# Layer 0's dense product in matmuls of 256 columns instead of 512

## What is computed

```python
def _L0_cond_ref(x, condition, weights):
    W = weights[condition]
    return jnp.einsum('bct,bcd->bdt', x, W)

def _L0_ffn_ref(x, W_base, b_base, enc0, enc1, coefs0, coefs1, mask0, mask1):
    base = jnp.einsum('bsd,od->bso', x, W_base) + b_base
    ...
    transformed = real_fourier_orthogonal_multiply(decoded)
    update = transformed.sum(axis=0)
    return base + update * SCALING

def _L1_ffn_ref(x, kernel, scale):
    w = kernel.astype(x.dtype) * 2.0 - 1.0
    return scale * jnp.einsum('bsi,if->bsf', x, w)

x = x + _L0_ffn_ref(_L0_cond_ref(x, itok_B_0_15, L0_cond_weights), ...)
x = x + _L1_ffn_ref(_L1_cond_ref(x, itok_B_0_30, L1_cond_weights), ...)
```

## Time and profile before

| | |
|---|---|
| median of 3 runs | 227.8 us (227.55 to 227.83) |
| profiled execution | 227.68 us |
| its span, first to last instruction | 225.5 us |
| TensorE busy (matmuls) | 220.1 us, 98%, 1212 records |
| weight loads | 185.2 us, 82%, 1212 records |
| POOL, DVE, ACT busy | 110.1, 98.8, 75.0 us |

### The profile page before, as it was taken

How to read it: one execution, slowest core, us unless ns; L and a number is a source line. 1 busy time by engine, 2 the same in 40 slices (tenths; PEclk the granted TensorE clock), 3 DMA queues, 4 the chain that set the end, 5 groups by cost and what they waited for, 6 DMA issues and landing times.

```text
span 225.5 us, 3597 instructions
## 1 busy us (share of the span) xinstructions
PE 220.1 (98%) x1212; PEld 185.2 (82%) x1212; DVE 98.8 (44%) x147; ACT 75.0 (33%) x199; POOL 110.1 (49%) x133
## 2 busy tenths in 40 slices
PE   7799999999999999999999999999999999999995
PEld 2568888888888888888888888888888888888884
DVE  4246444344544343445443444454434444544334
ACT  2067233333322333333223333332233333322211
POOL 4757754355566545445665454456654544522200
PEclk9999999999999999999999999999999999999999
DMA  6931022333222323322233323221232332212112
GB/s 201 310 99 52 9 96 96 102 93 84 72 53 96 99 96 99 99 63 88 52 96 99 96 99 99 71 81 52 96 99 96 99 99 81 73 49 90 47 49 93
DMA packets 13543, 20.42 MB, mean 91 GB/s; under 512 B 2618, under 2 KB 4538, under 8 KB 13538
## 3 DMA queue, kind: packets, MB, share of 16 engines
q1 hardware_dynamic: 10642, 18.16, 25.3%
q0 software_dynamic: 2048, 1.05, 2.4%
q10 hardware_dynamic: 848, 1.14, 1.5%
HBM read 11.96 MB, written 8.39 MB: 90 GB/s over the span
## 4 chain that ended last, share of the span: by engine, by line
PE 95%; DMA 3%; DVE 0%; ACTq 0%; issue 0%
PE f_ps L443 26%; PE y_ps L423 26%; PE f_ps L453 13%; PE f_ps L460 13%; PE f_ps L465 13%; DMA basis_sb<-in_fourier_basis 3%; PE a_ps L481 2%; PE a_ps L408 1%; PE y_ps L417 0%; DVE x L392 0%; PE a_ps L460 0%; PE f_ps L417 0%; PE a_ps L465 0%; ACTq L260 0%; ACTq L259 0%
## 5 line engine op out<-in xcount | busy, mean ns | idle before, releaser
L224 POOL TENSOR_TENSOR x<-x_in,bias 128x512 f32<-128x512 f32 x32 | 40.9, 1278 | 81.0 <-issue 46.9
L217 POOL DMA_INDIRECT gathered<-in_L_cond_weights,row_now x58 | 56.5, 974 | 13.2 <-issue 10.1
L443 PE MATMUL f_ps<-a_high,y_high 128*128 128x512 f32 x128 | 53.8, 420 | 0.0
L443 PE MATMUL f_ps<-a_low,y_high 128*128 128x512 f32 x128 | 50.3, 393 | 0.0
L358 DVE TENSOR_TENSOR x<-f_ps,x 128x512 f32<-128x512 f32 x32 | 22.1, 692 | 49.4 <-PE f_ps L443 47.9
L286 ACT ACTIVATE y_high<-y_ps 128x512 fp32r<-128x512 f32 x32 | 19.1, 597 | 69.6 <-PE y_ps L423 69.6
L282 ACT ACTIVATE y_high<-y_ps 128x512 fp32r<-128x512 f32 x32 | 19.1, 597 | 61.4 <-PE y_ps L423 61.4
L460 PE MATMUL f_ps<-b_sign,y_high 128*128 128x512 f32 x124 | 36.5, 415 | 0.0
L423 PEld LDWEIGHTS y_ps<-blocks,x_in 128*128 128x128 f32 x256 | 33.5, 191 | 3.5 <-issue 0.7
L423 PEld LDWEIGHTS y_ps<-blocks,x 128*128 128x128 f32 x256 | 33.4, 191 | 3.2 <-DVE x L358 0.5
L453 PE MATMUL f_ps<-a_high,y_low 128*128 128x512 f32 x128 | 35.1, 396 | 0.0
(11 more groups left out here) (44 smaller groups left out, 73.0 us busy)
## 6 DMA issues: line engine op xcount, KB each, us to landing
x_in<-in_x SPq DMA_DIRECT2D x31, 256.0 KB, 2.7
out_x<-x SPq DMA_DIRECT2D x31, 256.0 KB, 2.0
gathered<-in_L_cond_weights,row_now POOLq DMA_INDIRECT x58, 2.4
w_sb<-in_L_ffn_W_base SPq DMA_DIRECT2D x1, 512.0 KB, 7.5
w_sb<-in_L_ffn_W_base ACTq DMA_DIRECT2D x1, 512.0 KB, 8.9
basis_sb<-in_fourier_basis SPq DMA_DIRECT2D x1, 257.0 KB, 3.3
basis_sb<-in_fourier_basis ACTq DMA_DIRECT2D x1, 257.0 KB, 6.7
bias<-in_L_ffn_b_base SPq DMA_DIRECT2D x1, 256.0 KB
```

What stands on the lines that cost most here:

```text
L217: nc.gpsimd.indirect_dma_start(gathered[:, slot, layer, :], None, mix_rows[layer], IndirectOffsetOnAxis(rows[:, layer:layer + 1].bitcast(u ...
L224: nc.gpsimd.tensor_tensor(out=x1[:, slot, :], in0=x_in[:, slot, :], in1=bias[:, :], op=ALU.add).then_inc(biased, 1)
L443: last = nc.tensor.matmul(f0_ps[:, :], y0_high[:, k * P:(k + 1) * P], a[:, k, :], start=(k == 0 and a is a_high), stop=(k == CHUNKS - 1 an ...
```

## The change

Every matmul of feed0 becomes two, one for columns 0 to 255 and one for columns 256 to 511 of the same bank, of the same stationary operand. The list halves stood in the kernel already. Only the very first matmul of the two halves has start=True. Feed1 and everything else stays; the lines behind feed0 move down by four.

```diff
                     for a in (a_high, a_low):
-                        last = nc.tensor.matmul(f0_ps[:, :], y0_high[:, k * P:(k + 1) * P], a[:, k, :],
-                                                start=(k == 0 and a is a_high), stop=(k == CHUNKS - 1 and a is a_low))
+                        for half, columns in enumerate(halves):
+                            last = nc.tensor.matmul(f0_ps[:, columns], y0_high[:, k * P:(k + 1) * P], a[:, k, columns],
+                                                    start=(k == 0 and a is a_high and half == 0),
+                                                    stop=(k == CHUNKS - 1 and a is a_low), skip_group_check=True)
                     return last
 ...
                 for k in range(CHUNKS):
-                    nc.tensor.matmul(f0_ps[:, :], y0_low[:, k * P:(k + 1) * P], a_high[:, k, :], start=False, stop=False)
+                    for columns in halves:
+                        nc.tensor.matmul(f0_ps[:, columns], y0_low[:, k * P:(k + 1) * P], a_high[:, k, columns],
+                                         start=False, stop=False, skip_group_check=True)
                 high(CHUNKS - 1).then_inc(fed0, 1)
```

## The result

The changed kernel takes 225.69 us (median of 4 runs, 225.04 to 226.19), the kernel before 227.81 us beside it: a ratio of 0.990 with a 95% interval of 0.987 to 0.993. It is faster by 2.1 us, where 1.0 us slower was forecast, and outside the range. Most of what the forecast said of the mechanism is in the profile; the one price on which its sign hung is not. The kernel before takes 209.3 us from its first product on, so counted like this, too, the change is worth 2.1 us.

What follows compares the result with a forecast made beforehand. The prediction took TensorE's queue of matmuls, which never runs dry, as the bound: 227.68 us profiled + 1.07 for the splits = 228.75 us, 228.87 on the median's scale, stated as 228.8, range 226.9 to 231.0.

Steps and rivals of the forecast that it cites:

- the price of a half: Layer 0's product: a 256-column matmul with its load takes 117.75 ns, read in the last tile; a split costs 2.8 ns.
- the break-even: Layer 0's product: a half at 116.35 ns, half of 232.7 ns, below which the change makes the kernel faster.
- the faster rival: Layer 0's product: halves run at the loads' pace, about 113 ns; -2.6 us, 225.1 us; chance 0.12.
- its own tests: Wrong size if halves leave 117 to 119 ns; wrong mechanism if tiles outgrow the product or queue 8 brings blocks every turn.
- 1.07 us for all 12: Layer 0's product: 384 splits at 2.8 ns each, all on TensorE's path, add 1.07 us.
- The code was not brought in again: Slower rival, TensorE's loop: longer code fetched again at each of 8 returns, 8.8 us, 237.6 us; chance 0.04.
- the 7.4 us that it would give: Layer 0's product: if the load's estimated 107 ns alone paced the halves, the kernel would gain about 7.4 us.

Runs made afterwards that it cites:

- e0: The changed kernel run once more, with no edit, timed against the kernel before: 225.98 us, ratio 0.994.
- e13: The changed kernel with the last matmul of layer 0's product left whole: 228.56 us, ratio 1.003 to the kernel before.
- e14: e13 with the last chunk of layer 1's low part in two halves: 228.63 us, ratio 1.004 to the kernel before.
- the quarters: The changed kernel with layer 0's product in four parts of 128 columns instead of two halves: 309.02 us, one execution.
- e11: The changed kernel with both layers in halves, save the last matmul of each layer's product left whole: 224.58 us, ratio 0.987 to the kernel before.
- e12: e11 with one extra matmul, once, ahead of the loop: 224.42 us, ratio 0.986 to the kernel before.
- e3: The changed kernel with layer 1's product in interleaved halves too, in all tiles but the last: 227.04 us, ratio 0.997 to the kernel before.
- e7: e3 with the last low chunk of layer 1 left whole: 226.72 us, ratio 0.997 to the kernel before.
- e8: The changed kernel with the last chunk of layer 1's low part alone in two halves: 227.22 us, ratio 0.999 to the kernel before.

## Why the prediction was wrong

**The step that failed** is the price of a half: "I take the middle, 117.75 ns", and then "I stay at 117.75, since those rows are of the very operation, eight and six in a row". The rows were read rightly, and they were of the very operation, but from one stretch, 2 us at the end, entered after a wait of TensorE's load for y1_high, and the price was carried over to 31 tiles in a full queue. There a half takes 113 to 114 ns: the product is 2.74 us, 2.74 / 24 = 114.2 ns with its entry, so a split gains 232.7 - 228.3 = 4.4 ns and 384 of them 1.7 us. With the 0.01 us that layer 1's product is shorter in each tile (1.86 instead of 1.87 us), 0.3 us in all, that is the measured 2.1 us within the spread of the runs.

That the stretch read 118 seems to be partly luck of the one execution that was profiled: in the changed kernel the same stretch has read both ways. The halves of line 464 in the last tile, without the first and the last one, read as follows in its first profile and then in e0:

```profile
219.12 0.87 PE L464 MATMUL a_ps<-b_sign,y_high 128*128 128x256 f32 x6
```

```profile
217.90 0.84 PE L464 MATMUL a_ps<-b_sign,y_high 128*128 128x256 f32 x6
```

With 0.28 us for the last one this is (0.87 - 0.28) / 5 = 118 ns in one execution and (0.84 - 0.28) / 5 = 112 ns in the other, the better pace within the rounding of the rows. A single reading of this stretch could not give the price.

The term of the sum was thus mis-sized by 3.5 ns out of 118, and since the break-even lay at 116.35 ns, that turned the sign. The same stretch held the sign of the truth: "the last three spacings up to 221.52 us are 113 ns each". I made it the faster rival, "-2.6 us, 225.1 us", with 0.12, and it is what happened, within 0.6 us. I argued against it that "the six of line 465 show no spacing under 117 to 118"; two clusters of values in one stretch of the same operation were a sign of two paces, not of a spread around a middle, and the chances should have been split between them. By its own tests the forecast is wrong in its size and not in its mechanism.

**What the arithmetic was worth.** Where the slow pace holds, the forecast is near: e13 and e14 split 11 of the 12 matmuls of the same product, stand at 118 ns from the third tile on, and are 0.8 and 0.9 us slower than the kernel before, where I had 1.07 us for all 12. So the split is worth -2.1 us in the better pace and, by these two runs, about +0.8 us in the slower one.

**What held.** Every new matmul brings its load (1596 of each). All of the difference lies on TensorE's path. No wait took its place. The code was not brought in again: three blocks of queue 8 as before. So the rule of the Trainium skill, "Runtime: NRT & Kernel Launch", section "Instruction fetch mechanics", that a taken branch to a page outside a window of two has to fetch first, did not bite for this loop of 288 matmul and load records. Layer 1's product kept its 232 to 233 ns. The load's price by the Trainium skill, "TensorE: Matmul & The Clock Gate", section "LDWEIGHTS (loading the stationary operand)", an estimate of 107 ns for 128 columns, is near the 112 ns of the quarters and the 113 ns of the better pace. It pointed the right way, and the 7.4 us that it would give are more than three times the measured 2.1 us.

**What the first tile shows.** Its product ran at 118 ns, the second one changed to 113 ns within its first few matmuls, and all later ones ran at 113 ns. One product weighs little in the sum.

## What to carry to other kernels

When a change replaces an operation by another of which the trace has a few records, look at each record's start and not at their mean: two clusters can mean two paces, and the forecast needs a chance for each; a second profile of the same kernel can show whether the reading stands. Where TensorE ran fp32r matmuls with a fresh 128-column load each, the widest matmul was not always the cheapest per column: two of 256 columns were cheaper than one of 512 in the better pace (227 against 233 ns) and dearer in the slower one (236 ns). Leaving the last matmul of each product whole went with the better pace in both layers (e11, e12); leaving only layer 0's whole went with the slower one (e13). Check such a gain in the chain of every product that it touches, since an edit in one can change the pace of another.

## What the runs showed that was not expected

One matmul of 512 columns costs 233 ns, and two of 256 with two loads cost 227 in the better pace, so twice the loads can take less time. The pace of a run of halves, 113 or 118 ns from start to start, is set within its first few matmuls and then kept; it differs between two products of one tile (e3, e7), alternates between tiles (e7, e8), goes back after a disturbance (e12), and differs between two executions of one kernel in the last tile. The clock was granted in full throughout (0.998 to 1.000 over the span in all these runs), so it does not make the two paces. A matmul of 128 columns with its load costs 112 ns, about as much as a half in the better pace; 173 ns for one of 384 is an estimate.
